# Copying the row numbers of both tiles of a job in one GpSimd operation

## What is computed

```
s  = style @ mod_w.T + mod_b                 # per layer; the weights are modulated and demodulated
h  = four modulated 1-d convolutions of x    # same, up + blur, same, blur + down
scores = sigmoid(h @ gate_w.T) + bias        # 16 experts
topk_w, topk_idx = top_k(scores, 4);  topk_w /= sum(topk_w) + 1e-20
g, u = h @ Wg[e].T, h @ Wu[e].T              # H = 512, I = 256
out  = sum over the 4 chosen e of topk_w * (silu(g) * u) @ Wd[e].T
out += (silu(h @ Sg.T) * (h @ Su.T)) @ Sd.T
result = x + out
```

## Time and profile before

| | |
|---|---|
| timed runs | 1270.96, 1274.45, 1276.95 us; median 1274.45 |
| profiled execution | 1273.93 us, span of the profile 1272.2 us |
| busy: TensorE matmuls, weight loads, VectorE, ScalarE, GpSimd | 1158.0, 997.5, 857.5, 482.7, 570.5 us |
| GpSimd, gathers L406 | 140, 141.3 us |
| GpSimd, scatter-adds L420 | 140, 227.3 us |
| GpSimd, copies L453, L444, L431 | 138, 138, 140; 61.5, 55.0, 22.3 us |
| mean granted clock of TensorE | 0.974 |

### The profile page before, as it was taken

One profiled execution on the slowest core, in us unless ns is written; L12 is line 12 of the kernel. 1 busy time (PEld: TensorE's weight loads), 2 busy tenths in 40 slices (PEclk: granted clock), 3 DMA queues, 4 the chain that ended last, 5 costly groups with the idle time before them and its releaser, 6 DMA issues. The chain is left out here.

```text
span 1272.2 us, 26362 instructions
## 1 busy us (share of the span) xinstructions
PE 1158.0 (91%) x7065; PEld 997.5 (78%) x7066; DVE 857.5 (67%) x2456; ACT 482.7 (38%) x1087; POOL 570.5 (45%) x844
## 2 busy tenths in 40 slices
PE   4698999999999999982999999999999999999995
PEld 3576777777777776761998999999998889999995
DVE  8387788887878887865565565655656665555653
ACT  4354444544555445431333232322324332222321
POOL 0021222222222222233566657666666566666764
PEclk9699999999999999995999999999999999999998
DMA  4356444444444444422666766676766767666664
GB/s 153 90 131 178 125 122 124 130 124 130 127 128 129 128 129 126 121 76 97 144 117 150 128 148 115 118 158 120 154 119 154 186 113 156 124 109 116 111 112 79
DMA packets 115059, 162.24 MB, mean 128 GB/s; under 512 B 22880, under 2 KB 72096, under 8 KB 113504
## 3 DMA queue, kind: packets, MB, share of 16 engines
q0 software_dynamic: 35616, 74.08, 32.2%
q1 hardware_dynamic: 78128, 87.93, 24.4%
q10 hardware_dynamic: 1296, 0.01, 0.1%
HBM read 73.28 MB, written 55.18 MB: 101 GB/s over the span
## 5 line engine op out<-in xcount | busy, mean ns | idle before, releaser
L388 POOL DMA_INDIRECT lists<-entry,place x128 | 134.0, 1047 | 432.1 <-DVE place L791 400.9
L1183 PE MATMUL bank<-xt_hi,wup_hi 128*128 128x256 f32 x1104 | 272.0, 281 | 2.3 <-ACT xt_hi L599 1.5
L1183 PE MATMUL bank<-xt_hi,wup_lo 128*128 128x256 f32 x1104 | 272.3, 280 | 0.0
L420 POOL DMA_INDIRECT out_rows<-yb,sid x140 | 227.3, 1624 | 85.2 <-DVE yb L964 57.7
L1183 PEld LDWEIGHTS bank<-xt_hi,wup_hi 128*128 128x128 f32 x1104 | 209.1, 189 | 7.3 <-issue 2.4
L1183 PEld LDWEIGHTS bank<-xt_hi,wup_lo 128*128 128x128 f32 x1104 | 208.2, 189 | 2.9
L406 POOL DMA_INDIRECT xg<-h_rows,gid x140 | 141.3, 1009 | 95.9 <-PE bank L1161 37.1
L1187 PE MATMUL bank<-xt_lo,wup_hi 128*128 128x256 f32 x1104 | 174.2, 280 | 0.0
L964 DVE TENSOR_SCALAR yb<-bank,all_lists 128x512 f32<-128x512 f32 x138 | 101.2, 749 | 107.5 <-DMA out_rows<-yb,sid 74.7
L202 PE MATMUL bank<-x_hi,cwt_hi 128*128 128x512 f32 (+1 forms) x352 | 139.9, 400 | 15.2 <-DVE x_hi L836 11.6
L507 ACT ACTIVATE t<-bank,cB,cA 128x256 f32<-128x256 f32 x256 | 127.3, 570 | 63.2 <-PE bank L209 53.9
(11 more groups left out here) (208 smaller groups left out, 2133.0 us busy)
## 6 DMA issues: line engine op xcount, KB each, us to landing
x<-x1p SPq DMA_DIRECT2D x256, 64.0 KB
x<-x1p SPq DMA_DIRECT2D x256, 63.8 KB
wraw<-in_Wup SPq DMA_DIRECT2D x11, 1024.0 KB
xraw<-in_x SPq DMA_DIRECT2D x32, 256.0 KB, 2.6
xbase<-in_x SPq DMA_DIRECT2D x32, 256.0 KB
h_rows<-hrow SPq DMA_DIRECT2D x128, 64.0 KB
out_rows<-orow SPq DMA_DIRECT2D x32, 256.0 KB
wdraw<-in_Wdn SPq DMA_DIRECT2D x11, 512.0 KB
```

What stands on the lines that cost most here:

```text
L388: pool.indirect_dma_start(out=lists, out_offset=bass.IndirectOffsetOnAxis(ap=place[:, par, k:k + 1], axis=0), in_=entry[:, par, k, :], in_ ...
L420: pool.indirect_dma_start(out=out, out_offset=bass.IndirectOffsetOnAxis(ap=sid[:, u, :], axis=0), in_=yb[:, u, :], in_offset=None, compute ...
L1183: pe.matmul(dst, lhs[a], rhs[0], start=k == 0 and a == 0, stop=False)
```

## The change

GpSimd's two copies of one column each become one copy of two columns, in all five places: the first gather's row numbers, the next gather's, the scatter's, the next scatter's, and the padding ones at the start. The tiles `gid`, `sid` and `sid_next` change from shape 128x2x1 to 128x2. In `job` the copy to `gid` now comes behind the waits for both gathers of the job; before, each column's copy came behind the wait for its own gather. The semaphore counts halve accordingly. The gathers and scatter-adds themselves are still one per tile.

```diff
-        gid = sb("gid", [P, 2, 1], I32)
+        gid = sb("gid", [P, 2], I32)
 ...
-            for u in range(2):
-                pool.tensor_copy(gid[:, u, :], all_ids[:, u:u + 1]).then_inc(S["gather_id"], 1)
-            pool.wait_ge(S["gather_id"], 2)
+            pool.tensor_copy(gid[:], all_ids[:, 0:2]).then_inc(S["gather_id"], 1)
+            pool.wait_ge(S["gather_id"], 1)
 ...
             def add_last(j):
                 pool.wait_ge(S["b_added0"], 16 * (j + 1))
                 pool.wait_ge(S["b_added1"], 16 * (j + 1))
-                pool.wait_ge(S["scatter_id"], j * 4 + 2)
+                pool.wait_ge(S["scatter_id"], j * 2 + 1)
                 land(pool)
+                pool.tensor_copy(sid[:], sid_next[:]).then_inc(S["scatter_id"], 1)
                 for u in range(2):
-                    pool.tensor_copy(sid[:, u, :], sid_next[:, u, :]).then_inc(S["scatter_id"], 1)
-                for u in range(2):
-                    pool.wait_ge(S["scatter_id"], j * 4 + 4)
+                    pool.wait_ge(S["scatter_id"], j * 2 + 2)
                     pool.wait_ge(S["b_y"], j * 2 + (1 + u))
                     land(pool)
                     add(u)
 ...
             def job(j, here, ahead):
                 for u in range(2):
                     pool.wait_ge(S[f"b_gathered{u}"], 16 * (j + 1))
-                    land(pool)
-                    pool.tensor_copy(gid[:, u, :], all_ids[:, bass.ds(ahead + u, 1)]).then_inc(S["gather_id"], 1)
+                land(pool)
+                pool.tensor_copy(gid[:], all_ids[:, bass.ds(ahead, 2)]).then_inc(S["gather_id"], 1)
                 for u in range(2):
-                    pool.wait_ge(S["gather_id"], j * 2 + (3 + u))
+                    pool.wait_ge(S["gather_id"], j + 2)
                     pool.wait_ge(S["b_xt_t"], j * 2 + (1 + u))
                     land(pool)
                     gather(u)
                 add_last(j)
-                for u in range(2):
-                    pool.tensor_copy(sid_next[:, u, :], all_ids[:, bass.ds(here + u, 1)]).then_inc(S["scatter_id"], 1)
+                pool.tensor_copy(sid_next[:], all_ids[:, bass.ds(here, 2)]).then_inc(S["scatter_id"], 1)
 
-            for u in range(2):
-                pool.tensor_copy(sid_next[:, u, :], pad_i[:, u:u + 1]).then_inc(S["scatter_id"], 1)
+            pool.tensor_copy(sid_next[:], pad_i[:]).then_inc(S["scatter_id"], 1)
```

More of the change, by code:

```diff
@@ L172, in mk_adaln_ffn @@
         all_ids = sb("all_ids", [P, E * COLS], I32)
-        gid = sb("gid", [P, 2, 1], I32)
-        sid = sb("sid", [P, 2, 1], I32)
-        sid_next = sb("sid_next", [P, 2, 1], I32)
+        gid = sb("gid", [P, 2], I32)
+        sid = sb("sid", [P, 2], I32)
+        sid_next = sb("sid_next", [P, 2], I32)
         xg = sb("xg", [P, 2, H])
@@ L406, in gather @@
                 pool.indirect_dma_start(out=xg[:, u, :], out_offset=None, in_=h_rows,
-                                        in_offset=bass.IndirectOffsetOnAxis(ap=gid[:, u, :], axis=0)).then_inc(S[f"b_gathered{u}"], 16)
-            for u in range(2):
-                pool.tensor_copy(gid[:, u, :], all_ids[:, u:u + 1]).then_inc(S["gather_id"], 1)
-            pool.wait_ge(S["gather_id"], 2)
+                                        in_offset=bass.IndirectOffsetOnAxis(ap=gid[:, u:u + 1], axis=0)).then_inc(S[f"b_gathered{u}"], 16)
+            pool.tensor_copy(gid[:], all_ids[:, 0:2]).then_inc(S["gather_id"], 1)
+            pool.wait_ge(S["gather_id"], 1)
             for u in range(2):
@@ L419, in add @@
             def add(u):
-                pool.indirect_dma_start(out=out, out_offset=bass.IndirectOffsetOnAxis(ap=sid[:, u, :], axis=0),
+                pool.indirect_dma_start(out=out, out_offset=bass.IndirectOffsetOnAxis(ap=sid[:, u:u + 1], axis=0),
                                         in_=yb[:, u, :], in_offset=None, compute_op=ALU.add).then_inc(S[f"b_added{u}"], 16)
```

## The result

Over 20 runs of each, the changed kernel takes 1268.59 us (median, 1264.45 to 1272.84) and the kernel before 1275.04 us (1270.64 to 1280.73): a ratio of 0.9949, 95% interval 0.9937 to 0.9961, or 6.5 us less. The forecast was 2.45 us less, so the sign is right and the size is off by more than double. 1268.59 us lies in the stated range of 1266.5 to 1277.5, but outside of the bounds that I gave my own mechanism (1270.0 to 1273.5): the range reaches that low for the spread of the runs and for a rival.

What follows compares the result with a forecast made beforehand. TensorE was taken as the bound, GpSimd 0.84 us a job quicker. The start's 0.45 us and 2.0 us of TensorE's later waits sum to 2.45 us less: 1272.0 us from 1274.45, range 1266.5 to 1277.5.

Steps and rivals of the forecast that it cites:

- my own mechanism: Savings at the routed part's start and in TensorE's later waits: 1272.0 us, bounds 1270.0 to 1273.5, chance 0.45.
- The end: Last job's first scatter-add waits for yb, not for the row numbers: 0 us saved.
- The start: Copies ahead of the first gathers: one in place of two saves 0.45 us, bounds 0 and 0.55.
- a flip: At the start, tile 1's gather slips ahead of a weight load: up to 2.95 us more, second transpose by 598.5.
- transfers set everything: Under a weight load an earlier issue brings no earlier landing: 1274.0 us, chance 0.28.
- Slower: Earlier gathers meeting weight loads delay scatter-adds, yb, z and zt_hi: up to 12.8 us more, 1287.3 us, chance 0.05.
- the wide copy costs as much: A two-column copy costs as much as two narrow ones, no lap changes: 1274.45 us, chance 0.09.
- The term for the lap: GpSimd's merged copies in each job save 0.35 us, own-pace lap near 8.07 us in place of 8.42.
- The term (b): TensorE's 12 later waits in the routed part, 7.9 us, shrink by 2.0 us, bounds 0 and 7.9.
- The second rival: Scatter-adds and the start's second gather go ahead of weight loads: 11.3 us less, 1263.2 us, chance 0.13.
- its milder form: Half of the later waits' gain and tile 1's full gain at the start: 7.4 us less, 1267.1 us.
- the first rival: The 16 transfer engines are the bound under a weight load, earlier issue lands no earlier: 1274.0 us, chance 0.28.

Runs made afterwards that it cites:

- sid_only: The kernel before with only the copies to sid and sid_next merged; ratio 0.9952 to the kernel before.
- after_pad2: The changed kernel plus six spare one-column copies a job, two ahead of each wide copy; ratio 1.0092 to the kernel before.
- before_cut: The kernel before with each expert weight load of the routed part cut from 1.5 MB to 0.125 MB; ratio 0.9879 to the kernel before.
- after_pad1: The changed kernel plus three spare one-column copies a job, one ahead of each wide copy; ratio 0.9985 to the kernel before.
- after_landed: The changed kernel with weight loads issued only once the scatter-adds after the job that split the former weights have landed; ratio 0.9981 to the kernel before.
- after_late: The changed kernel with weight loads issued only once both scatter-adds of the job that split the former weights are issued; ratio 0.9949 to the kernel before.

## Why the prediction was right in sign and short in size

**Right.** The wide copy costs nothing more than a narrow one. The undisturbed lap is 9.26 us and the longer wait is for TensorE. The end gained nothing. The start gave 0.50 us where 0.45 was forecast (the copy took 0.50 us in place of 1.10, and the first gather starts 0.59 us sooner behind its start), and the second transpose did not slip ahead of the load (599.55 us, over the 598.5 named as the mark of a flip). The merged `gid` wait cost nothing. Two signs were missed by a little: the first transpose came at 594.80 us and not near 596.1 (0.67 us of that from before the change's first copy), and TensorE's later waits are 3.9 us, under the 4 to 7.5. Of the rivals, "transfers set everything" is out: the jobs gave 5.7 us. "Slower" did not come, and "the wide copy costs as much" is out.

**The term for the lap.** I summed 0.11 + 0.11 + 0.13 = 0.35 us and expected a lap of 8.07 us; it is 8.18. The `sid` pair's 0.24 us is there (8.42 to 8.18), and `sid_only` has it too. The 0.11 us for `gid` is zero, since the gather's start moved from 0.84 to 0.97 us behind the copy. I priced the copy by its end and not by the start of what follows it.

**The term (b), 2.0 us, measured 5.7.** This is the step that failed, in three places. First its ceiling. I took TensorE's waits as listed, 7.9 us, for all that could be won. Counted in laps against the kernel with cut loads, the loads cost the jobs 12.8 us before and 7.4 us after. The list of waits does not hold it all. Missing records are not the reason: 657 matmuls in 100 us against 733 in a full stretch is fewer jobs done, and a long lap has 67 to 69 matmul records like any other. But the page's ends of matmuls are modelled, and of the 3.31 us that the lap of 12.58 us is too long, the wait rows hold 2.57; where the rest lies is not shown. The listed waits fell from 7.9 to (5.2 - 3.7) + 2.4 = 3.9 us, by 4.0, itself double of what I gave (b).

Second, the saving per wait. I gave each wait one or two laps' saving and halved it for transfers. But GpSimd falls about 3 us behind with a load and recovers by the difference of the laps: 9.27 - 8.41 = 0.86 us a job before, 1.09 after, 0.42 in `after_pad2`, so by this estimate in about 3.5, 2.8 and 7 jobs. The traces bear it out where the loads are eight jobs apart (the third to the fifth): VectorE waits for scatter-adds in 4 or 5 jobs behind each of them before, in 3 after, and in every one until the next load in `after_pad2`. How often GpSimd has caught up, and waits for TensorE ahead of a gather, tells the same; before, changed, `after_pad2` (us in total, times, longest):

```profile
POOL xg L406 <- PE bank L1161: 37.1, 27, 3.6
```

```profile
POOL xg L406 <- PE bank L1156: 65.8, 45, 2.6
```

```profile
POOL xg L407 <- PE bank L1163: 5.8, 5, 1.7
```

Where the loads come after two to four jobs, the lag carries over to the next load and reaches VectorE's `yb`, `z`, `zt_hi` and TensorE. TensorE's excess over laps of 9.27 us, each from one profile:

| kernel | own-pace lap | laps 2 to 40 | laps 41 to 48 |
|---|---|---|---|
| `before_cut` | 8.39 | 0.5 | 0.0 |
| changed | 8.18 | 1.6 | 6.8 |
| before | 8.41 | 3.2 | 10.2 |
| `after_pad1` | 8.50 | 2.2 | 8.1 |
| `after_pad2` | 8.85 | 13.7 | 13.3 |

In `after_pad2` the lone loads cost as much as the dense ones, as they should where GpSimd needs seven jobs of the eight. The points are measured; that the lag adds up in this way is argued from them, and `after_pad1`, which has less excess than the kernel before at a longer lap, shows that the lap is not all. It has the 1.7 us head start at the load of the earlier trace rows.

Third, the order. I built two rivals on the one load in the earlier trace rows, which went out 0.78 us ahead of the second scatter-add, and took the wait of 4.05 us for that one's; it was the first one's, 1.31 us ahead of the load. This load is the exception: of the nine loads within the jobs, eight went out behind the start of the second add in the kernel before as well. What costs is the time that a scatter-add and a load share: `after_landed`, whose loads go out 5.8 to 6.7 us behind the start of the second add, takes VectorE's wait from 57.0 to 12.0 us. The second rival got near to the size (its milder form was 7.4 us). As I wrote it, with second adds going ahead of the loads and the second gather at the start ahead of its load, it did not happen; something of its kind did at one load, where the first add got away, for 0.9 us of TensorE's lap. That it was near in size is luck.

**The sharing of the engines.** A scatter-add beside a load holds the `sid` copy for 2 to 3 us longer than without one (8.05 and 7.13 against 4.93 us), and lands some 3 to 6 us later where landings were recorded. What the Trainium skill says ("Trainium Kernel Development and Optimization", section "Key Constraints"), that transfers from all queues run on the same engines and interleave, agrees with that. The result that I let the first rival draw from it, 1274.0 us, does not: the transfers beside a load do land late, but a shorter lap on GpSimd makes up for it sooner, and a scatter-add issued 0.4 us earlier against the load got past it once.

## What to carry to other kernels

Measure an engine's slack where it runs at its own pace, as lap against lap: an engine that is busy 45% of the time may be only 0.86 us a job ahead of the bound, and 0.24 us more is then over a quarter of its slack. Ask how long it takes to recover from each disturbance and how often the disturbances come; a cheap saving in the lap pays most where they come faster than it recovers. Where in the lap it is made can matter too: of two savings of 0.15 us, only the one ahead of the scatter-adds showed in the time. And count what can be won as laps over the undisturbed lap, not as the sum of the listed waits.

## What the runs showed of the hardware

A gather starts 0.97 us behind the end of the one wide copy of its row numbers, and 0.84 us behind the end of the second of two narrow ones: halving the copies saved nothing there. An accumulating scatter of 128 rows of 2 KB took 6.8 to 8.9 us from its descriptors to the `sid` copy that waits for it beside a 1.5 MB load (kernel before and changed), and 4.2 to 4.9 us with that load cut, where the copy waited for 0.8 us at most. Its landing, where recorded, came 2.8 to 4.0 us behind the end of its descriptors alone, and 6.5 to 9.1 us with the load issued between 1.1 us behind its start and 1.0 us ahead of it; with the load 1.7 us behind the start it came in 3.1 to 3.2 us. In the kernel before, the changed one and `after_late`, SyncE's loads went out 0.2 to 0.3 or 1.2 to 1.3 us behind the start of the second scatter-add in eight of nine cases; why they keep that distance was not looked into.
